# A macaron block of six windowed-attention layers run twice: one stream of units with the outer residual token-major, and the feed-forward statistics ahead of the probability sums on VectorE

## The reference

```python
x = x + 0.5 * ffn_stack(layernorm(x))
x = x + attn(layernorm(x))          # its softmax runs over an axis of length 1
x = x + 0.5 * ffn_stack(layernorm(x))

def ffn_stack(x):                   # 6 layers, the same weights in both calls
    for i in range(6):
        x = attn_layer(shift_tokens(x), Wqkv[i], q_scale[i], k_scale[i], Wo[i]) + x
        x = ffn_layer(shift_tokens(x), ln_g[i], ln_b[i], W1[i], b1[i], W2[i], b2[i]) + x
    return x
```

## Time and profile before

| | |
|---|---|
| median of 3 runs | 3177.44 us (3176.27 to 3177.71) |
| time of the profiled execution | 3177.99 us |
| span of the profiled execution, first to last instruction | 3176.2 us |
| time outside the span | 1.8 us |
| mean granted TensorE clock | 0.985 |
| PE, DVE, ACT, POOL busy share | 94%, 85%, 78%, 79% |

### The profile page before, as it was taken

How to read it: one execution, slowest core, us unless ns; L and a number is a source line. 1 busy time by engine, 2 the same in 40 slices (tenths; PEclk the granted TensorE clock), 3 DMA queues, 4 the chain that set the end, 5 groups by cost and what they waited for, 6 DMA issues and landing times.

```text
span 3176.2 us, 150320 instructions
## 1 busy us (share of the span) xinstructions
PE 2993.6 (94%) x63234; PEld 2516.1 (79%) x63234; DVE 2691.3 (85%) x4787; ACT 2469.2 (78%) x5064; POOL 2524.2 (79%) x2558
## 2 busy tenths in 40 slices
PE   6999999999999999999779999999999999999996
PEld 4788888878878888888657888888888788888885
DVE  4988888888899889988559888888988998898884
ACT  4888788778878887887548888887888788878885
POOL 5987888888788888887449888878887888888773
PEclk8999999999999999999889999999999999999998
DMA  2221222222222222222112222222222222222221
GB/s 85 77 64 48 77 65 54 68 70 52 68 70 57 66 67 62 65 67 54 34 28 78 61 57 71 65 52 73 69 52 67 74 52 71 61 62 53 57 52 38
DMA packets 117862, 195.44 MB, mean 62 GB/s; under 512 B 23756, under 2 KB 36552, under 8 KB 117192
## 3 DMA queue, kind: packets, MB, share of 16 engines
q1 hardware_dynamic: 117192, 185.82, 22.3%
HBM read 33.71 MB, written 1.05 MB: 11 GB/s over the span
## 4 chain that ended last, share of the span: by engine, by line
PE 65%; DVE 16%; issue 8%; ACT 6%; POOL 2%; DMA 0%; DVEq 0%; ACTq 0%; SPq 0%; POOLq 0%
PE of_ps L1010 8%; PE tr L1025 8%; PE s_ps L971 8%; DVE ss_floor L754 6%; PE tr L984 5%; PE tr L909 4%; PE of_ps L1068 4%; PE qk_ps L909 3%; PE qk_ps L911 3%; PE qk_ps L910 3%; PE tr L936 3%; PE tr L949 3%; PE tr L911 2%; PE tr L910 2%; DVE den L776 2%
## 5 line engine op out<-in xcount | busy, mean ns | idle before, releaser
L436 POOL TENSOR_TENSOR rotated<-rotated 128x1024 f32<-128x1024 f32 x384 | 914.9, 2383 | 22.6 <-DVE rotated L747 22.6
L463 POOL TENSOR_TENSOR rotated<-rotated,rn 128x1024 f32<-128x1024 f32 x384 | 730.8, 1903 | 30.1
L442 POOL TENSOR_TENSOR prob<-prob,rden 128x512 f32<-128x512 f32 x384 | 439.9, 1146 | 291.8 <-DVE rden L779 286.5
L548 ACT ACTIVATE sq<-qk_ps 128x1024 f32<-128x1024 f32 x384 | 393.8, 1025 | 169.7 <-PE qk_ps L911 94.1
L741 DVE TENSOR_TENSOR rotated<-qk_ps,rot 128x1024 f32<-128x1024 f32 x384 | 468.4, 1220 | 63.8 <-ACT sq L548 45.0
L747 DVE TENSOR_TENSOR rotated<-qk_ps,rot 128x512 f32<-128x512 f32 x768 | 490.9, 681 | 0.0
L754 DVE TENSOR_REDUCE ss_floor<-sq 128x16 f32<-128x1024 f32 x384 | 464.0, 1208 | 0.3
L1010 PE MATMUL of_ps<-pt,vs 64*64 64x32 f32 x12288 | 391.2, 222 | 35.3 <-DVE fstat L792 27.8
L1025 PE MATMUL tr<-ot,wo 128*128 128x128 f32 x3072 | 411.3, 277 | 1.1 <-issue 1.0
L1010 PEld LDWEIGHTS of_ps<-pt,vs 64*64 64x64 f32 x12288 | 326.0, 134 | 106.0 <-issue 49.0
L596 ACT ACTIVATE pt<-tr 128x512 f32<-128x512 f32 x384 | 229.8, 598 | 207.2 <-PE tr L984 206.7
(11 more groups left out here) (137 smaller groups left out, 6946.2 us busy)
## 6 DMA issues: line engine op xcount, KB each, us to landing
vs<-vn SPq DMA_DIRECT2D x384, 192.0 KB, 2.5
vs<-vtail SPq DMA_DIRECT2D x384, 64.0 KB, 2.0
vtail<-vn SPq DMA_DIRECT2D x384, 64.0 KB, 2.2
staging<-layer_wqkv_dram SPq DMA_DIRECT2D x72, 256.0 KB, 3.0
wo<-layer_wo_dram SPq DMA_DIRECT2D x12, 512.0 KB, 3.9
xs<-xa SPq DMA_DIRECT2D x48, 128.0 KB, 2.3
fs<-xa SPq DMA_DIRECT2D x48, 128.0 KB, 2.3
xs<-xa SPq DMA_DIRECT2D x48, 127.8 KB, 2.4
```

What stands on the lines that cost most here:

```text
L436: nc.gpsimd.tensor_tensor(rot_c[h], rot_c[h], rot_s[h], ALU.add).then_inc(rot_added, 1)
L442: nc.gpsimd.tensor_tensor(prob[h][:, :, :], prob[h][:, :, :], rden[h][:, :].unsqueeze(2).to_broadcast([P, 2 * PAIRS, KEYS]), ALU.mult).the ...
L463: nc.gpsimd.tensor_tensor(folded, folded, rn[:, :].unsqueeze(2).to_broadcast([P, 2 * UH, DH]), ALU.mult).then_inc(qkn_ready, 1)
```

## The change

Four things change.

1. The two passes become one stream of 384 units. The helpers of the slots lose their pass argument. The first units of the second stack are projected while the last feed-forward parts of the first are still under way.
2. The outer residual `x0` is kept token-major. For each sequence its own step adds half of the stack's result, takes the statistics, forms the token sum for the middle attention, adds the result of that, takes statistics again, whitens and turns the sequence into `xa`. For the middle of the kernel these steps are put into the slots of the next sequence's units, modulo 8 at 2 (`half_turn`), 3 (`half_sum`, `token_statistics`, `token_variance`, `token_deviation`), 4 (`token_sum`), 5 (`hidden_sum`, `mix`), 6 (`mixed_sum`, statistics again), 7 (`token_white`, `turn`) and 0 (`token_back`). At the end only `half_turn` and `half_sum` are left, and each sequence is written by a DMA of its own. The two weight matrices of the middle attention are multiplied once into `mixT` in slots 3 to 6.
3. The start no longer transposes the input. DVE takes the statistics of each sequence as it arrives, and the first splits of the weights move from POOL to DVE (`first_low`), in the order that the first unit needs them. The constants have semaphores of their own.
4. In slot 4 modulo 8 `statistics` stands ahead of `prob_sums` on DVE.

The core of the diff on DVE and PE, with the new functions:

```diff
+            def token_statistics(s, k):
+
+                for c in range(TPS):
+                    last = nc.vector.bn_stats(xstat[:, c, :], x0[:, s, c, :])
+                last.then_inc(xstat_ready, 1)
+
+            def token_variance(k):
+                dve.wait_ge(xstat_ready, k + 1)
+                for c in range(TPS):
+                    last = nc.vector.bn_aggr(xmoment[:, c, :], xstat[:, c, :])
+                last.then_inc(xmoment_ready, 1)
...
+                nc.vector.tensor_scalar(x_minus_mean[:, :], xmoment[:, :, 0], -1.0, None, ALU.mult)
+                nc.vector.tensor_scalar(xvar[:, :], xmoment[:, :, 1], EPS, None, ALU.add).then_inc(xvar_ready, 1)
+
+            def token_white(s, k, i):
+
+                dve.wait_ge(xshift_ready, k + 1)
+                if i > 0:
+                    dve.wait_ge(xturned, i)
+                for c in range(TPS):
+                    last = nc.vector.tensor_scalar(xwhite[:, c, :], x0[:, s, c, :], xrstd[k % 2][:, c:c + 1], xshift[k % 2][:, c:c + 1],
+                                                   ALU.mult, ALU.add)
+                last.then_inc(xwhite_ready, 1)
+
+            def token_back(s, i, src):
+
+                dve.wait_ge(xturned, i + 1)
+                nc.vector.tensor_scalar(xa[:, s, :], src, 1.0, None, ALU.mult).then_inc(mac_ready, 1)
+
+            def half_sum(j):
+
+                dve.wait_ge(half_ps, j + 1)
+                halves = x0[:, j % SEQS, :, :].rearrange("p (a c) d -> p a (c d)", a=2)
+                nc.vector.scalar_tensor_tensor(halves, f_ps, 0.5, halves, ALU.mult, ALU.add).then_inc(half_added, 1)
...
+            def mixed_sum(s):
+                dve.wait_ge(mix_ps, s + 1)
+                nc.vector.tensor_tensor(x0[:, s, :, :], tr1[:, 0:P].unsqueeze(1).to_broadcast([P, TPS, P]), x0[:, s, :, :], ALU.add
+                                        ).then_inc(mix_added, 1)
...
-            for p in range(PASSES):
-                if p == 0:
-                    dve.wait_ge(x0_ready, SEQS)
-                macaron_ln(2 * p * SEQS)
-                tokens_low(p * SEQS * DEPTH)
...
+            for n in slots:
+                if (s := mid_of(n, SUM_AT + 1)) is not None:
+                    hidden_sum(s)
+                if (j := half_of(n, HALF_AT + 1)) is not None:
+                    half_sum(j)
+                if (s := mid_of(n, MIXED_AT)) is not None:
+                    mixed_sum(s)
+                if (s := mid_of(n, OUT_AT)) is not None:
+                    dve.wait_ge(mix_added, s + 1)
+                    token_white(s, SEQS + 2 * s + 1, SEQS + s)
+                if (s := mid_of(n, BACK2_AT)) is not None:
+                    token_back(s, SEQS + s, tr1[:, :])
+                if (it := ffn_of(n, STATS_AT)) is not None:
+                    statistics(it)
+                if live(n - 1):
+                    prob_sums(n - 1)
...
+            def half_turn(j):
...
+                    last = nc.tensor.transpose(f_ps[:, c // 2, c % 2 * P:(c % 2 + 1) * P], xa[:, s, c * P:(c + 1) * P], ident[:, :])
...
+            def token_sum(n, s):
...
+                for c in range(TPS):
+                    nc.tensor.matmul(tr1[:, 0:1], x0[:, s, c, :], xrstd[k % 2][:, c:c + 1], start=c == 0, stop=False)
+                for c in range(TPS):
+                    last = nc.tensor.matmul(tr1[:, 0:1], ones[:, :], xshift[k % 2][:, c:c + 1], start=False, stop=c == TPS - 1)
...
+                if (j := half_of(n, HALF_AT + 1)) is not None:
+                    pe.wait_ge(half_added, j + 1)
```

More of the change, by code:

```diff
@@ new lines, in build @@
+        xmoment_ready = sem("xmoment_ready")
+        xvar_ready = sem("xvar_ready")
+        xrstd_ready = sem("xrstd_ready")
+        xshift_ready = sem("xshift_ready")
+        xwhite_ready = sem("xwhite_ready")
+        xturned = sem("xturned")
+        mac_ready = sem("mac_ready")
+        half_ps = sem("half_ps")
+        half_added = sem("half_added")
+        hsum_ps = sem("hsum_ps")
+        hsum_ready = sem("hsum_ready")
+        mix_ps = sem("mix_ps")
+        mix_added = sem("mix_added")
@@ L902, in project, with mix @@
+            def mix(n, s):
+                pe.wait_ge(pt_ready, ONE + n)
+                pe.wait_ge(hsum_ready, s + 1)
+                pe.wait_ge(mixt_ready, 1)
+                nc.tensor.matmul(tr1[:, 0:P], hsum[:, 0:1].to_broadcast([P, P]), mixT[:, :], start=True, stop=True).then_inc(mix_ps, 1)
             def project(dst, U, part):
@@ new lines, in _ @@
+            for s in range(SEQS):
+                turn(s, start_ps[s])
+            for n in slots:
+                after_gated = (it := ffn_of(n - 1, GATED_AT)) is not None
+                if after_gated and not live(n):
+                    pe.wait_ge(hid_ready, ONE + 2 * NCH * (it + 1))
+                if live(n + 2):
+                    project_qk(n + 2)
+                if live(n):
+                    query_heads(n)
+                    key_heads(n)
+                if live(n - 2):
+                    weigh_values(n - 2)
+                if live(n):
+                    project_v(n)
+                    scores(n)
+                if (it := ffn_of(n, DOWN_AT)) is not None:
+                    down(n, it)
+                if live(n - 1):
+                    prob_major(n - 1)
+                if live(n - 2):
+                    project_out(n - 2)
+                if (it := ffn_of(n, TURN_AT)) is not None:
+                    if (j := half_of(n, HALF_AT + 1)) is not None:
+                        pe.wait_ge(half_added, j + 1)
+                    token_major(it)
+                if (it := ffn_of(n, BACK_AT)) is not None:
+                    feature_major(it)
+                if (it := ffn_of(n, GATED_AT)) is not None:
+                    gated(n, it)
+                if (j := half_of(n, HALF_AT)) is not None:
+                    half_turn(j)
+                if (s := mid_of(n, SUM_AT)) is not None:
+                    token_sum(n, s)
+                if (s := mid_of(n, MIX_AT)) is not None:
+                    mix(n, s)
+                if (s := mid_of(n, OUT_AT)) is not None:
+                    pe.wait_ge(pt_ready, ONE + n)
+                    turn(SEQS + s, tr1[:, :])
+                if n == 3:
```

645 lines of the change are left out of this document (317 added, 328 removed).

## The result

The changed kernel takes 3105.05 us (median of 4 runs, 3103.55 to 3105.9) against 3176.86 us, a ratio of 0.9774 (95% interval 0.9757 to 0.9791): faster by 72 us. Its profiled execution took 3104.9 us, with a span of 3103.1.

A forecast was written before the change was run, and what follows sets the result against it. PE was taken as nearly full in two long stretches, with losses at the joint and both ends. Terms -50.2 + 2.0 - 16.5 - 4.8 - 14 = -83.5 us took 3178.0 to 3094.5, given as 3094, range 3066 to 3122.

The forecast's parts named there:

- The joint: Between the passes: 76.6 us go, 26.4 return as middle steps, 6.6 for each of four sequences; net -50.2 us.
- the collision: Middle slots: whitening on DVE runs into POOL's addition, 1.5 us a sequence, bounds 0 and 4.8.
- ACT and DVE set the pace there, so I count 0.3: Middle slots 4 and 5: PE's token sum, put at 0.9 us, is mostly covered; 0.3 us a sequence is paid.
- The last layer: half_sum and half_turn fall into two live sequences' slots, 0.69 and some 0.3 us each: +2.0 us.
- The start: Before the first rotation: DVE's list brings it to 29.6 us instead of 46.05, -16.5 us, bounds -20 and -11.
- The end: Behind the last add_ffn: shorter work and a quarter-size transfer take 5.4 us instead of 10.2, -4.8, bounds -3.5 and -5.5.
- The statistics first: Slot 4 modulo 8: PE's 0.6 us wait goes, DVE gains 0.30 us for each of 46 occurrences: -14 us.
- The first, dearer steps: Joint: the steps cost 12 us a sequence instead of 6.6, giving 3116 us; chance 0.17.
- The second: Slot 4: the reordering gives nothing or loses a little through POOL's late scaling, 3108 to 3117 us; chance 0.12.
- the third: Slot 4: the reordering gives PE's full wait, 3080 us; chance 0.10.
- the fourth: Slot 4: the late reciprocal holds POOL, then PE, through the group; slower than before, 3180 us at the earliest; chance 0.02.
- The fifth, the clock: Joint's slots: PE's clock falls to its lower level in 10 us of each sequence, +24, so 3118 us; chance 0.06.

The follow-up runs named there:

- the sums first: The changed kernel with the four bn_stats of slot 4 put back behind the probability sums: 3122.82 us, ratio 0.9827 to the kernel before.
- The early start: The changed kernel with sequence 0 whitened before sequence 1 arrives and unit 0 projected behind the first turn: 3098.26 us, ratio 0.9753 to the kernel before.

## Why the prediction was right

3094 us was forecast (3066 to 3122) and 3105 measured: right in sign, place and range, 11 us too low by sizes.

1. **What bounds the kernel.** Right. There are two stretches with PE full, a joint and two ends; the two full stretches changed by 4.4 us in 1192 and 6.0 in 1252.
2. **The joint.** Forecast -50.2, measured -44.3: it stood 77.1 us above steady groups and stands 32.8 above them now. With the sums first the same reckoning gives 38.2, so some 5 of the 44.3 hang on the reordering, and the joint's own part is nearer 39. Slot 3 was over-sized (2.2 against 1.5 us), and the rest beside slots 4 and 5 was right as a sum (2.6 + 1.5 against 4.1), the collision in it measured at 1.66 with PE's wait behind it. (In the earlier trace rows, from which its price came, POOL's addition ends at 880.90 and not at 881.3; DVE's instruction ends at 881.46.) The step that failed is "ACT and DVE set the pace there, so I count 0.3" for slots 4 and 5: 2.4 us were paid up to slot 6's rotation, some of it mixed_sum's 0.7. PE's token sum is on the chain, as its shortening shows, and it takes 1.84 us, not 0.9, since each fp32 matmul is two rows in the trace and 16 rows are 8 matmuls.
3. **The last layer.** Forecast +2.0; the intervals from slot 2's rotation to slot 3's that hold it are 0.4 us longer (6.62 against 6.21), twice.
4. **The start.** Forecast -16.5, measured -11.2, at the edge of its bounds. The list was right, its prices too low: whitening 1.1 to 1.5 us and not 0.8, a wait of 1.2 to 1.3 us for each turn, the third whitening 2.1 us longer beside a memset, and 3.8 us from the first projection to the rotation where 2.7 were taken (the first matmuls of 512 columns take 0.63 us there, 0.40 in the steady part). The early start shows that VectorE's list and the fourth turn set the first rotation, and that they set unit 24's only in part.
5. **The end.** -4.8 forecast; behind the last add_ffn it is 4.9 us instead of 10.2, -5.3. The terms of the forecast add up to 5.15 us and not 5.4, so by its own terms it was -5.05.
6. **The statistics first.** Forecast -14, measured -11.2 alone and -17 to -18 in the changed kernel. "For each of 46" is the step that failed: in three of four sequences the gain is about 0.3 to 0.4, in the fourth nothing, since minus_mean runs into POOL's instruction. In the joint it is worth 6.8 us more: PE starts 0.8 us earlier in each middle slot 4, and the lower clock, some 4 us in all, does not come there. That the joint saved less than forecast and the reordering more is in part luck for the sum.
7. **The rivals.** The first, dearer steps, was the true direction (8.2 us a sequence, between 6.6 and 12). The second, the third and the fourth (no gain, the full wait, a loss) lie outside the interval of the reordering alone. The fifth, the clock, came in small: two falls in slot 7, 1 us in all, where 24 were its price. With the four instructions in the old order it is four falls in slot 4 and some 4 us.

## What to carry to other kernels

A short element-wise instruction of VectorE that runs beside GpSimd should be read by its longest time, not by its mean: where the longest ends with GpSimd's instruction, another form of the same operation (a reduction over one element, a scalar operation that also writes a sum) takes the wait away, and moving it to ScalarE or moving GpSimd's work may only move the wait. A reordering's gain should be estimated for each class of slot by itself, since one class can have a collision that swallows it. Here it was worth most where PE's idle time was longest, and where a fall of the clock came on top of the wait. A fall of a few us does not show in the page's row of slices; the windows behind PE's longest waits have to be asked for. What is moved out of the first unit's way at the start has to be out of the second's too.

## What the runs showed of the hardware

- A tensor_scalar on 4 columns between SBUF tiles waits for a running POOL instruction as one on 128 columns does: up to 1.35 us instead of 0.16. As a tensor_reduce it never took more than 0.157, and the tensor_scalar with a row sum never more than 0.407.
- A POOL memset, which only writes, holds such an instruction up too: at the start of the changed kernel the longest whitening instruction takes 2.52 us instead of 0.34, from 24.19 to 26.72, and POOL runs nothing but memsets from 24.33 on.
- Not every POOL instruction holds it. Beside POOL's power on 4 columns (18.17 to 19.20 in the changed kernel) four whitening instructions (18.00 to 19.11) keep 0.34 us each.
- With PE idle for 1.78 to 1.98 us in slot 4 the granted clock was 0.50 to 0.64 in the 2 us windows read about 1 us behind it, in four places of four of the one profiled execution. Behind 1.69 to 1.84 us in slot 7 it fell 6 times of 24, in six profiled executions, and behind 2.04 to 2.08 us in another kernel's slot 7 never in four. What makes the difference was not tried.
